# First expert layer of a four-layer network: units of 256 and of 128 token rows in place of units of 256 alone

## What is computed

```python
probs = jax.nn.softmax(flat @ router_w, axis=-1)
topw, topi = jax.lax.top_k(probs, TOP_K)                       # TOP_K = 2, E = 8
combine = jnp.sum(jax.nn.one_hot(topi, E) * topw[..., None], axis=1)
h = jax.nn.silu(jnp.einsum('td,edf->tef', flat, w1) + b1)      # 128 -> 512
y = jnp.einsum('tef,efd->ted', h, w2) + b2                     # 512 -> 128
out = jnp.einsum('te,ted->td', combine, y)
```

## Time and profile before

| | |
|---|---|
| median of 3 runs | 1468.93 us |
| lowest and highest run | 1465.43 and 1472.74 us |
| profiled execution, span from first to last instruction | 1467.0 us |
| profiled execution, own time beside its span | not listed apart; the span lies 1.9 us under the median |
| mean granted TensorE clock over the span | 0.895 |
| PE, DVE, ACT and POOL busy over the span | 80%, 67%, 45% and 37% |
| first hidden product and last result of the unit stage | 333.3 and 516.9 us |

### The profile page before, as it was taken

How to read it: one execution, slowest core, us unless ns; L and a number is a source line. 1 busy time by engine, 2 the same in 40 slices (tenths; PEclk the granted TensorE clock), 3 DMA queues, 4 the chain that set the end, 5 groups by cost and what they waited for, 6 DMA issues and landing times. The chain is left out here.

```text
span 1467.0 us, 34935 instructions
## 1 busy us (share of the span) xinstructions
PE 1171.7 (80%) x11141; PEld 918.1 (63%) x11154; DVE 988.9 (67%) x2920; ACT 667.1 (45%) x1423; POOL 538.9 (37%) x590
## 2 busy tenths in 40 slices
PE   2699994439999957779987879999799956499991
PEld 1477773338899925556673456677477755399991
DVE  3689996474443347998984679888477777766552
ACT  1367762105555503345564546766234343144440
POOL 2324201664235256534411232431121125752554
PEclk9999997559999967899998989999799988599996
DMA  6887743012223258435532177564200042133542
GB/s 179 206 215 191 188 124 129 29 33 87 77 92 109 75 133 209 122 101 144 150 84 51 44 176 167 150 163 106 86 1 0 0 152 74 53 120 106 149 140 73
DMA packets 138978, 164.58 MB, mean 112 GB/s; under 512 B 15308, under 2 KB 118754, under 8 KB 131728
## 3 DMA queue, kind: packets, MB, share of 16 engines
q1 hardware_dynamic: 130664, 146.62, 37.0%
q0 software_dynamic: 8192, 16.46, 4.1%
HBM read 111.98 MB, written 51.38 MB: 111 GB/s over the span
## 5 line engine op out<-in xcount | busy, mean ns | idle before, releaser
L586 DVE TENSOR_REDUCE A_neg_max<-A_s_bank 128x4 f32<-128x512 f32 x384 | 253.2, 688 | 46.3 <-PE A_s_bank L725 35.9
L448 ACT ACTIVATE A_probsT<-A_st_bank 128x512 f32<-128x512 f32 x384 | 222.4, 602 | 40.4 <-PE A_st_bank L738 39.2
L725 PE MATMUL A_s_bank<-A_k_stack,A_q_stack 72*128 72x128 bf16 x1536 | 157.5, 228 | 38.0 <-DVE A_neg_max L586 22.3
L738 PE MATMUL A_st_bank<-A_q_stack,A_k_stack 128*128 128x128 bf16 x1536 | 153.1, 224 | 7.1 <-DVE A_q_stack L602 6.2
L738 PEld LDWEIGHTS A_st_bank<-A_q_stack,A_k_stack 128*128 128x128 bf16 x1536 | 112.5, 103 | 52.2 <-issue 42.9
L725 PEld LDWEIGHTS A_s_bank<-A_k_stack,A_q_stack 72*128 72x128 bf16 x1536 | 106.3, 102 | 52.1 <-DVE A_neg_max L586 33.4
L752 PE MATMUL A_pv_bank<-A_probsT,A_v_pad 128*32 128x128 f32 x3072 | 127.4, 284 | 1.5 <-issue 1.5
L2041 ACT ACTIVATE E_h<-E_h_bank,w_L_b 128x256 f32<-128x256 f32 x184 | 76.8, 471 | 72.4 <-PE E_h_bank L2141 71.0
L2153 PE MATMUL E_y_bank<-E_w,E_h 128*128 x736 | 90.3, 276 | 2.2 <-ACT E_h L2041 0.9
L752 PEld LDWEIGHTS A_pv_bank<-A_probsT,A_v_pad 128*32 128x32 f32 x3072 | 74.1, 111 | 24.7 <-issue 3.4
L2141 PE MATMUL E_h_bank<-E_xT,E_w_u 128*128 128x256 f32 x368 | 88.8, 386 | 0.0
(11 more groups left out here) (371 smaller groups left out, 2641.4 us busy)
## 6 DMA issues: line engine op xcount, KB each, us to landing
A_q_stack<-q_scratch SPq DMA_DIRECT2D x48, 576.0 KB
A_k_stack<-k_scratch SPq DMA_DIRECT2D x32, 576.0 KB
q_scratch<-A_q_parts SPq DMA_DIRECT2D x48, 192.0 KB, 2.3
A_k_stack<-k_scratch SPq DMA_DIRECT2D x48, 192.0 KB
E_xe<-slots_in SPq DMA_DIRECT2D x53, 128.0 KB, 2.1
slots_out<-E_ye SPq DMA_DIRECT2D x53, 128.0 KB, 1.7
A_ctxT<-in_ctxT SPq DMA_DIRECT2D x24, 256.0 KB, 10.5
k_scratch<-A_k_parts SPq DMA_DIRECT2D x32, 192.0 KB
```

Of the source, the lines that this page charges most:

```text
L448: act.activation(probsT[n % 2][:, c * HQ:(c + 1) * HQ, :], st_bank[c % 2][:, :].rearrange("k (a q) -> k a q", a=HQ), ACT.Exp, scale=scale) ...
L586: dve.tensor_reduce(neg_max[:, c * HQ:(c + 1) * HQ], s_bank[c % 2][:, :].rearrange("q (a k) -> q a k", a=HQ), AX.X, ALU.max, negate=True). ...
L725: last = pe.matmul(s_bank[c % 2][:, a * S:(a + 1) * S], q_stack[slot][0:COMBO, h, at:at + S], k_stack[slot][0:COMBO, h, at:at + S], start= ...
L738: last = pe.matmul(dst, k_stack[slot][:, h, at:at + S], q_stack[slot][:, h, at:at + S], start=True, stop=spread)
```

## The change

Each part now has 16 units of 256 rows and eight of 128 rows, 24 in all, 48 in both parts. For each expert `table` takes whole units while more than 128 rows are left, up to 16 in the part (`cut`, `taken`), and puts what is left into units of 128 (`left`). The order of the work is fixed: two units of 256, one of 128, eight times a part (`column`, `rows_of`). Every step of a unit works on `rows_of[u]` rows; the weight copy and the register loads are the same for both sizes. Result rows depend on five terms per expert in place of three (`pieces_of_experts`, 22 DVE steps of eight elements, in rounds 1 and 19; they replace the five steps at `table`'s end), and `out_rows` works on five. The first `add_result` moves from round 25 to 27. Every other round number is unchanged.

```diff
-    UT = 256
-    unit_counts = [2 * (last - first) * CT // UT + NE - 1 for first, last in PARTS]
+    UT, ST = 256, 128
+    wholes = [2 * (last - first) * CT // UT for first, last in PARTS]
+    unit_counts = [n + NE for n in wholes]
     first_units = [sum(unit_counts[:p]) for p in range(len(PARTS) + 1)]
     NU = max(unit_counts)
     last_unit = first_units[-1]
+    column, rows_of = [], []
+    for p, n in enumerate(wholes):
+        for e in range(NE):
+            for i in (*range(e * n // NE, (e + 1) * n // NE), n + e):
+                column.append(first_units[p] + i)
+                rows_of.append(UT if i < n else ST)
...
-    ADDS = {0: 25}
+    ADDS = {0: 27}
...
+    def out_row(u):
+        p = part_of_unit[u]
+        i = column[u] - first_units[p]
+        return min(i, wholes[p]) * UT + max(i - wholes[p], 0) * ST
...
+                n = rows_of[u]
+                at = sp.value_load(row_of[0:1, column[u]:column[u] + 1], min_val=0, max_val=slots_in.shape[0] - UT)
+                sp.dma_start(xe[u % XBUF][:, 0:n // S, :], slots_in[bass.ds(at, n), :].rearrange("(p j) d -> p j d", j=n // S))\
...
+                    for i, size in enumerate((UT, ST)):
+                        own.did(dve.tensor_scalar(lims[:, i, :], held[:, :], -float(size), 0.0, ALU.add, ALU.max))
                     own.link(dve.tensor_tensor(square[:, :, :], held[:, :, None].to_broadcast([S, NE, MOST]),
                                                steps[:, None, :].to_broadcast([S, NE, MOST]), ALU.is_gt))
-                    own.link(dve.tensor_reduce(units[:, :], square[:, :, :], AX.X, ALU.add))
-                    own.link(dve.tensor_tensor(square[:, :, 0:NE], upto[:, :, :],
-                                               units[:, None, :].to_broadcast([S, NE, NE]), ALU.mult))
-                    own.link(dve.tensor_reduce(ends[:, :], square[:, :, 0:NE], AX.X, ALU.add))
+                    own.did(dve.tensor_reduce(counts[:, 0, :], square[:, :, :], AX.X, ALU.add))
+                    own.link(dve.tensor_reduce(counts[:, 1, :], square[:, :, 1::2], AX.X, ALU.add))
+                    own.link(dve.tensor_tensor(sums[:, :, :, :], upto[:, None, :, :].to_broadcast([S, 2, NE, NE]),
+                                               counts[:, :, None, :].to_broadcast([S, 2, NE, NE]), ALU.mult))
+                    own.link(dve.tensor_reduce(ends[:, :, :], sums[:, :, :, :], AX.X, ALU.add))
+                    own.link(dve.tensor_scalar(cut[:, 1:], ends[:, 1, :], float(w), None, ALU.min))
+                    own.did(dve.tensor_tensor(taken[:, :], cut[:, 1:], cut[:, 0:NE], ALU.subtract))
+                    own.link(dve.scalar_tensor_tensor(left[:, 1:], cut[:, 1:], -2.0, ends[:, 0, :], ALU.mult, ALU.add))
                 if 1 in pieces:
-                    own.link(dve.tensor_tensor(hit, per_u(ends[:, :]), per_e(numbers), ALU.is_le))
+                    for of, many, until in kinds:
+                        own.did(dve.tensor_tensor(hit[:, of, :], per_u(until, many), per_e(numbers[:, 0:many], many), ALU.is_le))
+                    own.wait()
...
+                    own.link(dve.tensor_tensor(taken_hit[:, :, :], hit[:, w:n, :], per_u(taken[:, :], NE), ALU.mult))
+                    own.did(dve.tensor_reduce(skipped[:, :], taken_hit[:, :, :], AX.X, ALU.add))
...
-                    own.did(dve.scalar_tensor_tensor(terms[:, p, 2, :], units[:, :], float(UT), lim[:, :], ALU.mult, ALU.subtract))
-                    own.did(dve.tensor_tensor(terms[:, p, 1, :], lim[:, :], begins[:, p, :], ALU.add))
-                    own.link(dve.tensor_tensor(terms[:, p, 0, :], ends[:, :], units[:, :], ALU.subtract))
...
                     dve.sem_inc(table_done, 1)
+            def pieces_of_experts(p):
+
+                begin, threshold, step, second, second_step = (terms[:, p, i, :] for i in range(5))
+                after, far = float(wholes[p] * UT), 4.0 * TOK
...
+                own.link(dve.tensor_tensor(second_step, second_step, step, ALU.subtract))
+                own.link(dve.scalar_tensor_tensor(step, cut[:, 0:NE], -float(UT), step, ALU.mult, ALU.add))
             def out_rows(c):
 
+                p = part_of_chunk[c]
                 for k in range(2):
                     own.did(dve.tensor_tensor(weighed[:, :, k * RT:(k + 1) * RT, :],
-                                              pick[:, k:k + 1, chunk(c), :].to_broadcast([S, 3, RT, NE]),
-                                              terms[:, part_of_chunk[c], :, None, :].to_broadcast([S, 3, RT, NE]), ALU.mult))
+                                              pick[:, k:k + 1, chunk(c), :].to_broadcast([S, 5, RT, NE]),
+                                              terms[:, p, :, None, :].to_broadcast([S, 5, RT, NE]), ALU.mult))
...
+                for i in (1, 3):
+                    own.did(dve.tensor_tensor(chosen[:, i, :, :], slot[:, :, chunk(c)], chosen[:, i, :, :], ALU.is_ge))
+                own.wait()
+                for i in (1, 3):
+                    own.did(dve.tensor_tensor(chosen[:, i, :, :], chosen[:, i, :, :], chosen[:, i + 1, :, :], ALU.mult))
+                own.wait()
+                own.link(dve.tensor_tensor(chosen[:, 0, :, :], chosen[:, 0, :, :], chosen[:, 1, :, :], ALU.add))
+                own.link(dve.tensor_tensor(index_out[:, :, chunk(c)], chosen[:, 0, :, :], chosen[:, 3, :, :], ALU.add))
...
+                if u == 1:
+                    pieces_of_experts(0)
                 if located in (1, 2, 3):
                     table(1, (located - 1,))
+                if located == 9:
+                    pieces_of_experts(1)
...
-                for j in range(2):
+                for j in range(rows_of[u] // S):
...
-                        dst = h_bank[(2 * u + q) % HB][:, f % 2 * UT:(f % 2 + 1) * UT]
-                        last = pe.matmul(dst, w1_u[u % WBUF][:, f * 128:(f + 1) * 128], xT[u % 3][:, :],
+                        dst = h_bank[(2 * u + q) % HB][:, f % 2 * n:(f % 2 + 1) * n]
+                        last = pe.matmul(dst, w1_u[u % WBUF][:, f * 128:(f + 1) * 128], xT[u % 3][:, 0:n],
...
-                for j in range(2):
+                for j in range(rows_of[u] // S):
```

More of the change, by code:

```diff
@@ L1577, in routed_ffn @@
         held = sb("held", [S, NE])
-        lim = sb("lim", [S, NE])
+        lims = sb("lims", [S, 2, NE])
         square = sb("square", [S, NE, MOST])
-        units = sb("units", [S, NE])
-        ends = sb("ends", [S, NE])
+        counts = sb("counts", [S, 2, NE])
+        sums = sb("sums", [S, 2, NE, NE])
+        ends = sb("ends", [S, 2, NE])
+        cut = sb("cut", [S, 1 + NE])
+        left = sb("left", [S, 1 + NE])
+        many = sb("many", [S, NE])
+        other = sb("other", [S, NE])
+        taken = sb("taken", [S, NE])
+        taken_hit = sb("taken_hit", [S, NE, NE])
+        skipped = sb("skipped", [S, NE])
         passed = sb("passed", [S, NU, NE])
@@ L1849, in table @@
                 first, last = PARTS[p]
-                n, at = unit_counts[p], first_units[p]
-                per_u = lambda v: v[:, None, :].to_broadcast([S, n, NE])
-                per_e = lambda v: v[:, :, None].to_broadcast([S, n, NE])
-                numbers = core.iota_units[:, 0:n]
+                w, n, at = wholes[p], unit_counts[p], first_units[p]
+                kinds = ((slice(0, w), w, cut[:, 1:]), (slice(w, n), NE, left[:, 1:]))
+                per_u = lambda v, n: v[:, None, :].to_broadcast([S, n, NE])
+                per_e = lambda v, n: v[:, :, None].to_broadcast([S, n, NE])
+                numbers = core.iota_units
                 hit = passed[:, 0:n, :]
@@ L1869, in table @@
                     own.did(dve.tensor_copy(expert_of[:, at:at + n], which[:, 0:n]))
-                    own.did(dve.tensor_tensor(begun[:, 0:n], numbers, begun[:, 0:n], ALU.subtract))
+                    for of, many, _ in kinds:
+                        own.did(dve.tensor_tensor(begun[:, of], numbers[:, 0:many], begun[:, of], ALU.subtract))
+                    own.wait()
                 if 2 in pieces:
-                    own.link(dve.tensor_tensor(hit, per_u(core.iota8[:, :]), per_e(which[:, 0:n]), ALU.is_equal))
@@ L1875, in table @@
+                    for i, (of, many, _) in enumerate(kinds):
+                        own.did(dve.tensor_tensor(hit[:, of, :], hit[:, of, :], per_u(lims[:, i, :], many), ALU.mult))
+                    own.wait()
+                    own.did(dve.tensor_reduce(row[:, 0:n], hit, AX.X, ALU.add))
                     own.did(dve.tensor_scalar(which[:, 0:n], which[:, 0:n], float((last - first) * REGION),
                                               float(first * NE * REGION), ALU.mult, ALU.add))
-                    own.link(dve.scalar_tensor_tensor(row[:, 0:n], begun[:, 0:n], float(UT), row[:, 0:n], ALU.mult, ALU.min))
+                    own.link(dve.scalar_tensor_tensor(begun[:, w:n], skipped[:, :], 2.0, begun[:, w:n], ALU.mult, ALU.add))
@@ L1878, in table @@
```

(8 more changed lines are left out.)

72 lines of the change are left out of this document (43 added, 29 removed).

## The result

The changed kernel took 1463.22 us (median of 20 runs, 1456.81 to 1468.21), the kernel before 1472.21 beside it (20 runs): a ratio of 0.9936, interval 0.9923 to 0.9949, so 9.0 us of medians and 9.4 by the ratio. A second comparison, on another chip, gave 1459.93 against 1472.93, 0.9921 (0.9904 to 0.9939). The forecast was 11.7 less, or 1457.2. The median lies 6.0 above that; 3.3 of it is the kernel before, at 1472.21 here against 1468.93 in the three runs that the forecast started from.

The account below looks back on a forecast made before the run. The unit stage was taken as bound by TensorE, busy 30.00 of 30 us. Terms: -22.0 tensor work, +1.4 table, +7.9 DVE in part 0, +1.0 register loads, together -11.7, giving 1457.2 us; range 1450 to 1465.

Parts of the forecast that it names:

- Tensor work: Unit stage on TensorE: a 128-row unit takes 1.89 us, half of a whole unit's time; minus 22.0 us.
- The rival of weight loads: Small hidden products: weight loads set their pace, 1.52 in place of 0.89, sixteen times; +10.1 us, 1467.3; chance 0.05.
- Table: Start of the stage: the longer table(0) on DVE delays the first transposes, none of it hidden; plus 1.4 us.
- Early places: Part 0, rounds 1, 6 and 10: PE comes earlier but waits for DVE, 0.84 us each; plus 2.5 us.
- Rounds 13 to 15: Part 0: DVE's table piece and two out_rows take 12.75 us against tensor rounds of 9.35; plus 2.9 us on PE.
- Rounds 19 to 21: Part 0: DVE's pieces_of_experts(1) and two out_rows outlast the tensor rounds; plus 2.5 us.
- Register loads: Small results: only 0.89 us of products in which to fetch the next unit's number; plus 1.0 us, from 0 to 3.
- Scatter: Ahead of part 1: its first load at 416.4, landed by 420.0, transposes at 420.7; hidden by less than 1 us.
- The warning that a quicker DVE: Rounds 13 to 15: if DVE were quicker there, the scatter would take most of that gain back.
- DVE kept up: Rival, part 0: only the early 2.5 and about 1 for the scatter remain, no register cost; -17.1 us, 1451.8; chance 0.17.
- its lateness did not double: Rival: DVE's lateness costs double, each late copy delaying the next; +7.9, so -3.8 us, 1465.1; chance 0.12.
- the one result bank: Rival, small units in both parts: results wait for the previous result's copy, making the kernel slower; 1476 and more; chance 0.05.

Follow-up runs that it names:

- The wide kernel: Changed kernel, but TensorE and ScalarE work on 256 columns for small units too; 1485.45 us, ratio 1.0068 to the kernel before.
- the doubled piece: Changed kernel with the first of the three pieces of part 0's table computed twice; 1458.81 us in one run.
- the blocks halved: Changed kernel with DVE's blocks (table's last third, part 1's terms, result rows) cut in two over twice as many rounds; 1455.38 us, ratio 0.9901.
- the kernel with the pace of eight: Against the blocks halved: scatter of chunks 2 and 3 waits for earlier transfers at every eighth, not fourth; 1452.37 us, ratio 0.9885 to the kernel before.
- moving the blocks whole: Changed kernel with part 1's terms and chunks 2 and 3's result rows in later rounds: 1462.31 us, 0.9931; all chunks' rows later: 1461.11 us, 0.9916.

## Why the prediction was right, step by step

- **Tensor work, -22.0.** A trio takes 9.36 or 9.37, as worked out (9.35): 46 x 3.73 less 16 x 9.36 is 21.8. The wide kernel, in which ACT's steps are long again too, shows that nothing else brings the gain: without the shorter products the change costs 0.7%. The rival of weight loads that set the pace (0.19 for each product) falls: eight products of 128 columns take 0.89, 0.111 each, and eight of 256 columns 1.73, 0.216 each. The Trainium skill, page "TensorE: Matmul & The Clock Gate", section "Back-to-back issue gap", has about 81 ns a product at 128 columns and 131 at 512 in streams of weight load and product; the float32 products of this trace do not follow that, they take time in proportion to their columns.
- **Table, +1.4.** Its length, the five terms counted before, grew from 5.48 to 6.75, 1.27, and 1.27 reached the first transposes. Size and step ("none of it hides") were right; the doubled piece, which arrived whole, shows that the table is on the path.
- **Early places, +2.5.** The three places named (`E_z`, `E_r`, `E_chosen`) lost 0.79, 0.94 and 0.83, 2.6. A fourth was missing: from result 8 to 9 the 0.89 saved shrank to 0.10, with ACT late behind its exponential and its table load. The prediction had costed ACT at nothing, because it is idle 13 of 30 us. So from result 0 to 11 50.38 became 47.32: 3.1 saved of the 6.5 that the tensor rounds got shorter, 3.4 lost. That ACT's lateness is the cause there is read from the trace alone; no run moved it.
- **Rounds 13 to 15, +2.9.** Their waits sum to 2.85 at rounds 15 to 17; with the blocks halved results 11 to 18 start 21.57 apart in place of 25.21, so 3.6: the DVE rounds took 4.49, 4.23 and 4.53, 13.25 for the 12.75 worked out, the first of them with 1.26 ahead of its weight copy. **Rounds 19 to 21, +2.5:** 1.66 of waits; from result 18 to 24, 21.13 against 18.73 in the kernel with the pace of eight, 2.4. The two, 5.4 predicted, are 6.0. The mechanism was the one stated, a DVE round longer than the tensor round that covers it; the halving shows it, as moving the blocks whole did not help.
- **Register loads, +1.0.** None of it on PE: part 1's trios have 9.36 and no gap. Their price lay on DVE, which the term had not in mind: 0.8 us at the end of each block, inside the length of its rounds.
- **Scatter.** Hidden, as predicted, with room: 5.43 lie between part 1's load and its use, and a load and its use were 3.63 apart before. In this trace the table's first step stands 1.57 later than in that of before, so times are counted from it: the load came 116.0 behind it (119.0 before, 116.4 predicted), the transposes 121.5 (122.6 before, 120.7 predicted). The terms of the prediction's sum for the transposes add up to 420.6, not 420.7. The warning that a quicker DVE would lose most of rounds 13 to 15 again was too dark: with DVE quick the scatter took back 1.0 of 6.0 (168.15 against 167.13), and the pace of eight avoids that.
- **Sum.** From the table's first step to the end of the last result 216.85 and 217.49 became 205.55 and 205.51: -11.3 and -12.0, against -11.7. By the terms as measured: -21.8 + 1.3 + 3.4 + 6.0 + 0 = -11.1. That the sum comes this close is in part luck: the register loads were 1.0 too dear, the missing ACT place 0.8 and rounds 13 to 15 0.7 too cheap.
- **Rivals.** DVE kept up only where its blocks were halved; its lateness did not double; the one result bank cost nothing in part 1 but the wait of the last result, which was there before.

## What to carry to other kernels

When tensor rounds get shorter, compare each round of the other engines with the round that covers it, not their sums: an engine with a third of its time idle made PE wait because some of its rounds took 4.2 to 4.5 us where a tensor round takes 2.84 to 3.62. Such a block is best cut in two and laid on more rounds; moved whole it gained 0.3 us at best, and with the order inside its rounds changed 3.88 of 4.51 us of waits were left. Look also for an engine's short chains: ACT, idle 13 of 30 us, was late in a round in which it changes its table. Judge such edits by a stretch inside the trace, since whole runs scatter by several us, and take a second trace of each kernel: here the stretch repeated within 0.1 us after the change and 0.8 before it.
